# A causal attention block with a quantized linear layer on eight cores: chunk 0's O tiles get a place each, and its attention starts after half of the projections

## What is computed

```python
Q, K, V = (split_heads(x @ W.T, 16) for W in (WQ, WK, WV))       # 16 heads of 64
scores = einsum('bhqd,bhkd->bhqk', Q, K) / 8;  causal mask;  attn = softmax(scores)
x1 = layernorm(x + einsum('bhqk,bhkd->bhqd', attn, V) @ WO.T)
x_q = round(rms_norm(x1) * 127 / absmax) / (127 / absmax)        # per row, clipped to int8
out = layernorm(x1 + x_q @ (w_int8 * weight_scale).T + bias)
```

## Time and profile before

| | |
|---|---|
| median of 3 runs | 1007.29 us (1006.96 to 1008.47) |
| the profiled execution: its own time | 1006.75 us |
| its span (core 1, the slowest; others 999.1 to 1003.6) | 1004.6 us |
| PE busy | 901.4 us, 90% of the span |
| ACT busy | 677.8 us, 67% |
| DVE busy | 524.4 us, 52% |
| POOL busy | 226.8 us, 23% |
| mean DMA rate | 71 GB/s |

### The profile page before, as it was taken

One profiled execution on the slowest core, in us unless ns is written; L12 is line 12 of the kernel. 1 busy time (PEld: TensorE's weight loads), 2 busy tenths in 40 slices (PEclk: granted clock), 3 DMA queues, 4 the chain that ended last, 5 costly groups with the idle time before them and its releaser, 6 DMA issues.

```text
span 1004.6 us, 22672 instructions; the slowest of 8 cores (999.1 to 1004.6 us)
## 1 busy us (share of the span) xinstructions
PE 901.4 (90%) x8416; PEld 416.6 (41%) x8416; DVE 524.4 (52%) x1269; ACT 677.8 (67%) x707; POOL 226.8 (23%) x289
## 2 busy tenths in 40 slices
PE   3895999999999999899999999999899998888863
PEld 1342444444444444444444444444344444444431
DVE  0110147834875337752148727862577523676665
ACT  0133756777787788888834666777677778989931
POOL 5022422322222111211122322232122111121201
PEclk9997999999999999999999999999999999999987
DMA  9999141530132122241071331141313210123222
GB/s 125 149 177 205 32 54 33 106 106 12 34 85 80 49 33 48 59 106 48 7 96 38 95 117 23 47 133 54 49 33 106 80 33 9 31 65 100 59 58 63
DMA packets 99289, 71.18 MB, mean 71 GB/s; under 512 B 70384, under 2 KB 88816, under 8 KB 99184
## 3 DMA queue, kind: packets, MB, share of 16 engines
q1 hardware_dynamic: 78368, 50.87, 19.7%
q0 software_dynamic: 20816, 18.88, 14.2%
HBM read 55.05 MB, written 16.78 MB: 71 GB/s over the span
## 4 chain that ended last, share of the span: by engine, by line
PE 68%; DMA 9%; ACT 7%; DVE 6%; issue 6%; DVEq 2%; POOL 1%; POOLq 0%; ACTq 0%; SPq 0%
PE ps L322 43%; PE ps L628 13%; PE ps L529 13%; ACT PT L557 6%; DMA WV<-wvt 4%; DMA QO<-OS 3%; DVE OS L664 2%; DMA XT<-xt 1%; ACT Q L826 1%; DVE SM L760 1%; DVE Z L890 1%; DMA QT<-QB 1%; DVEq L663 1%; DVE SM L757 1%; DVE SM L763 1%
## 5 line engine op out<-in xcount | busy, mean ns | idle before, releaser
L557 ACT ACTIVATE PT<-ps,SM 128x1024 bf16<-128x1024 f32 (+2 forms) x576 | 580.6, 1066 | 179.2 <-PE ps L529 176.2
L572 POOL TENSOR_TENSOR PT<-PT,MASK 128x256 bf16<-128x256 bf16 (+1 forms) x184 | 158.2, 867 | 540.0 <-ACT PT L557 539.9
L628 PEld LDWEIGHTS ps<-VX,PT 128*128 128x128 bf16 x4352 | 186.9, 98 | 185.0 <-issue 125.0
L628 PE MATMUL ps<-VX,PT 128*128 128x65 bf16 x4352 | 231.5, 194 | 29.2 <-DVE OS L664 28.5
L529 PE MATMUL ps<-QO,KT 64*128 64x512 bf16 (+1 forms) x1504 | 186.1, 324 | 23.7 <-ACT PT L557 20.6
L322 PE MATMUL ps<-XT,WK 128*128 128x512 bf16 x512 | 131.6, 383 | 19.2 <-DMA XT<-xt 18.9
L322 PE MATMUL ps<-W,QT 128*128 128x512 bf16 x512 | 135.2, 382 | 14.8 <-DMA QT<-QB 14.5
L322 PE MATMUL ps<-WO,QO 128*128 128x512 bf16 x512 | 134.8, 378 | 3.7 <-issue 2.2
L322 PE MATMUL ps<-WV,XT 128*128 128x512 bf16 x512 | 129.6, 385 | 3.9 <-DMA WV<-wvt 3.3
L322 PE MATMUL ps<-XT,WQ 128*128 128x512 bf16 x512 | 131.5, 378 | 0.6 <-DMA WQ<-wqt 0.6
L529 PEld LDWEIGHTS ps<-QO,KT 64*128 64x128 bf16 x1504 | 53.9, 94 | 174.2 <-issue 167.9
(11 more groups left out here) (50 smaller groups left out, 549.1 us busy)
## 6 DMA issues: line engine op xcount, KB each, us to landing
Z<-x SPq DMA_DIRECT2D x32, 512.0 KB, 4.1
y<-Z SPq DMA_DIRECT2D x32, 512.0 KB, 3.1
XT<-xt POOLq DMA_DIRECT2D x7, 1024.0 KB, 11.9
WK<-wkt POOLq DMA_DIRECT2D x4, 512.0 KB, 20.4
WQ<-wqt POOLq DMA_DIRECT2D x4, 512.0 KB, 23.3
WV<-wvt POOLq DMA_DIRECT2D x2, 1024.0 KB, 41.2
WO<-wot POOLq DMA_DIRECT2D x1, 2048.0 KB, 68.2
W<-w8t POOLq DMA_DIRECT2D x1, 2048.0 KB, 83.3
```

Source lines behind the costliest of these rows:

```text
L557: emit("s", lambda eng: eng.activation(dst, src, AF.Exp, bias=EB, scale=0.125).then_inc(sem["s"], 1))
L572: emit("g", lambda eng: eng.tensor_tensor(blk, blk, msk, ALU.mult).then_inc(sem["m"], 1))
L628: last = eng.matmul(ps[:, 2048 + s_ * 512 + q * 65: 2048 + s_ * 512 + q * 65 + 65], PT[:, pt0 + s_ * 512 + c0: pt0 + s_ * 512 + c0 + 128], ...
```

## The change

It has four parts.

1. **Order of the loads.** WK and WQ come in slices of 128, 256, 256 and 384 columns (head pair 0; 1 and 2; 3 and 4; 5 to 7) in place of four of 256. V's first half is loaded after the second slices, V's second half after the fourth ones, still ahead of XT1, WO and W8. Only WK's first slice lies between the two halves of x^T.
2. **Fewer fills ahead of attention.** Ahead of the first unit come K and Q of head pairs 0 to 2 and V's first half, 10 fills. The other 14 go first in the list that is spread over chunk 0's gaps: K and Q of pair 3, V's second half (4 fills), then K and Q of pairs 4 to 7.
3. **A place for each O.** Chunk 0's head pairs 0 and 1 use OS, 2 and 3 use O6 (the place of Q16/QB), 4 to 7 use QT8; both are idle in chunk 0. The wait for the transpose of pair i-2 is gone in chunk 0.
4. **Later first rows.** The loads of x and the bias are issued ahead of unit pair 8 of 12 of chunk 0. In chunk 1 four K fills are listed ahead of the first two row blocks' WO fills.

```diff
@@ -88,6 +88,7 @@
 
         Q16 = at("Q16", [128, 1024], F16, "q16")
         QB = at("QB", [128, 1024], BF16, "q16")
+        O6 = at("O6", [128, 1024], BF16, "q16")
         QT8 = at("QT8", [128, 2048], BF16, "qt8")
         BIAS = at("BIAS", [128, 1024], F32, "bias")
         MASK = at("MASK", [128, 128], BF16, "mask")
@@ -163,19 +164,20 @@
 
         tok_xt = {}
         tok_w = {}
+
+
         x0a = xt_load(XT0, 0, 0, 4, "x0a")
-        tok_w["k", 0] = wslice(wk_h, WK, 0, 256, "wk0")
-        x0b = xt_load(XT0, 0, 4, 8, "x0b")
-        tok_w["q", 0] = wslice(wq_h, WQ, 0, 256, "wq0")
+        for j, (i0, i1) in enumerate(((0, 1), (1, 3), (3, 5), (5, 8))):
+            for w, w_h, W in (("k", wk_h, WK), ("q", wq_h, WQ)):
+                tok = wslice(w_h, W, 128 * i0, 128 * i1, "w%s%d" % (w, j))
+                for i in range(i0, i1):
+                    tok_w[w, i] = tok
+                if (w, j) == ("k", 0):
+                    x0b = xt_load(XT0, 0, 4, 8, "x0b")
+            if j == 1:
+                tok_w["v", 0] = wslice(wv_h, WV, 0, 512, "wv0")
+        tok_w["v", 1] = wslice(wv_h, WV, 512, 1024, "wv1")
         tok_xt[0] = (x0a, x0b)
-        for j in range(1, 4):
-            tok_w["k", j] = wslice(wk_h, WK, 256 * j, 256 * j + 256,
-                                   "wk%d" % j)
-            tok_w["q", j] = wslice(wq_h, WQ, 256 * j, 256 * j + 256,
-                                   "wq%d" % j)
-        for j in range(2):
-            tok_w["v", j] = wslice(wv_h, WV, 512 * j, 512 * j + 512,
-                                   "wv%d" % j)
         tok_xt[1] = (xt_load(XT1, 1, 0, 8, "xt"),)
         tok_w["o"] = wslice(wo_h, WO, 0, 1024, "wo")
         tok_w["8"] = wslice(w8_h, W8, 0, 1024, "w8")
@@ -377,7 +379,7 @@
                     lambda kk: W[:, kk * 1024 + i * 128:
                                  kk * 1024 + i * 128 + 128],
                     lambda kk: X[:, kk * 512:kk * 512 + 512],
-                    lambda: (tok_w[which, i // 2],) + tok_xt[g])
+                    lambda: (tok_w[which, i],) + tok_xt[g])
 
             def done(n):
                 en = evac_engine(state["g"])
@@ -651,9 +653,14 @@
                 pv_end = t_tok()
                 later(2000.0, lambda: xt5_load(pv_end))
             wait("v", t_tok())
-            if i >= 2:
+            if su:
                 wait("v", tok_ot[(i - 2) // 8, (i - 2) % 8])
-            o0 = (i % 2) * 512
+            out, o_row, o0 = OS, 1024, (i % 2) * 512
+            if su == 0 and i >= 2:
+
+
+                out, o_row, o0 = ((O6, 1024, (i - 2) * 512) if i < 4 else
+                                  (QT8, 2048, (i - 4) * 512))
             r0 = 168 + (i % 2) * 8
 
             def f(eng):
@@ -662,7 +669,7 @@
                                   (65, nq)))
                 eng.drain()
                 eng.tensor_tensor(
-                    ap(OS, o0, (1024, 128), (64, 2), (128, nq), (1, 64)),
+                    ap(out, o0, (o_row, 128), (64, 2), (128, nq), (1, 64)),
                     ap(ps, 2048, (4096, 128), (512, 2), (65, nq), (1, 64)),
                     ap(SM, r0, (256, 128), (4, 2), (1, nq), (0, 64)),
                     ALU.mult).then_inc(sem["v"], 1)
@@ -675,7 +682,7 @@
             key = "ot%d" % (i % 2)
             emit("y", lambda eng: eng.dma_start_transpose(
                 ap(QO, c0, (8192, 128), (128, nq), (1, 128)),
-                OS[:, o0:o0 + nq * 128]).then_inc(sem[key], 16))
+                out[:, o0:o0 + nq * 128]).then_inc(sem[key], 16))
             tok_ot[su, hp] = bump(key, 16)
             if hp == 7:
                 later(5500.0, lambda: state["ot_all"].add(su))
@@ -837,7 +844,7 @@
             later(2200.0, lambda: bg.insert(0, (400.0, integers)))
 
             def resid(j):
-                wait("v", tok_q16[n], tok_bias)
+                wait("v", tok_q16[n], tok_bias[0])
                 z = zt(n, j * 512, j * 512 + 512)
                 emit("v", lambda eng: eng.scalar_tensor_tensor(
                     z, z, sm(n, 6, 7), BIAS[:, j * 512:j * 512 + 512],
@@ -965,29 +972,30 @@
         state["ot_all"] = set()
 
         tok_consts2 = [None]
+        tok_bias = [None]
 
 
         ops["v"] = vhead
         emit("v", consts_fn)
         tok_consts2[0] = bump("v")
 
-        for i in range(8):
+        for i in range(3):
             main.append(proj_filler("k", 0, i))
             main.append(proj_filler("q", 0, i))
-        for dc in range(2):
-            for r in range(4):
-                main.append(v_filler(0, r, dc))
+        for r in range(4):
+            main.append(v_filler(0, r, 0))
         while main or st["open"]:
             step()
 
-
-        wait("y", t_tok())
-        for n in range(NZ):
-            x_load(n)
-        emit("y", lambda eng: eng.dma_start(
-            BIAS[:, :], ap(bias_h, 0, (0, 128), (1, 1024))
-        ).then_inc(sem["bi"], 16))
-        tok_bias = bump("bi", 16)
+        def first_rows(t):
+
+            wait("y", t)
+            for n in range(NZ):
+                x_load(n)
+            emit("y", lambda eng: eng.dma_start(
+                BIAS[:, :], ap(bias_h, 0, (0, 128), (1, 1024))
+            ).then_inc(sem["bi"], 16))
+            return bump("bi", 16)
 
         def chunk_list(g):
 
@@ -1016,6 +1024,8 @@
                          v[0], ff[2], v[1], v[2], v[3], ff[3],
                          v[4], v[5], v[6], v[7], q[0], q[1], q[2], q[3]]
                 late = [q[4], q[5], q[6], q[7]]
+                if g == 1:
+                    order = order[2:6] + order[:2] + order[6:]
             return sum(order, []), sum(late, [])
 
         def behind(tiles):
@@ -1024,7 +1034,12 @@
             fl += [ffn_filler(n, dc) for n in tiles for dc in range(2)]
             return fl
 
+
         carry = []
+        for i in range(3, 8):
+            carry += [proj_filler("k", 0, i), proj_filler("q", 0, i)]
+            if i == 3:
+                carry += [v_filler(0, r, 1) for r in range(4)]
         pairs = {}
         for p in range(len(units) // 2):
             pairs.setdefault(subs[units[2 * p][0]][0], []).append(p)
@@ -1072,6 +1087,8 @@
                 fill(left() / max(1, gaps[0]))
                 gaps[0] -= 1
             for p in pairs[g]:
+                if p == pairs[0][8]:
+                    tok_bias[0] = first_rows(t_tok())
                 emit_s(2 * p)
                 emit_s(2 * p + 1)
                 pv_pair(p - 1, gap)
```

## The result

The changed kernel takes 1019.35 us in the median (1018.77 to 1019.62 in the three executions that are compared); its ratio to the kernel before is **1.0111, 95% interval 1.0093 to 1.0129**: slower by some 11 us. The forecast was 1008.1, its range 1005.2 to 1011.0.

A forecast was written before the change was run, and what follows sets the result against it. PE, busy 90% of the span, was taken to bound the kernel, with the DMA engines full for the first 100 us. 1006.75 - 0.2 + 0.6 + 0.4 = 1007.55, plus 0.54 for the median, gave 1008.1 us, range 1005.2 to 1011.0.

The forecast's parts named there:

- T - S + 20.2 - W: Time change past chunk 0's waits: S is the first score matmuls, W chunk 0's old wait; -0.2 us on core 1.
- The new wait: In chunk 0, PE stands from 41.2 to 54.7 us for V's second half, about 13.5 us.
- The wait of chunk 0: PE's wait in chunk 0 for a multiply of O, itself held by a transpose, goes: -10.3 us.
- Slices of 128 columns: Loads of WK and WQ: smaller packets make V's second half land +0.6 us later, between 0 and +2.7.
- rival A: 256-byte packets cost as much as 512-byte ones or more, so V's second half lands later: 1010.2 us, chance 0.20.
- Evacuations: In chunk 0, ACT evacuates 34 fills, not 20, between the same exps: +0.4 us, bounds 0 and 4.4.
- rival B: In chunk 0, fills are evacuated on ACT behind two exps: 1012.1 us at the upper bound, chance 0.13.
- Row loads later, and chunk 1's K fills first: 0: Later loads of x and bias in chunk 0, and K fills ahead of WO fills in chunk 1, cost 0.
- One of my own signs: In the changed kernel's profile, the first WO fill at about 134 us as before; wrong if over 3 us off.
- The cores: Core 1 -0.2 us, core 5 +0.4, core 2 +2.7; the longest span stays core 1's or core 5's.
- So the end costs what it did: At the kernel's end, the last 140 pieces of PE's order are the same, so its cost is unchanged.
- Rivals C and D: C: no slow restart behind PE's wait, 1005.6 us, chance 0.09. D: V's second half lands before PE asks, 993.6, 0.04.

The follow-up runs named there:

- e4: The kernel before with only the separate places for chunk 0's O; 994.21 us, ratio 0.9879 to the kernel before.
- e3: The changed kernel with V's second-half fills listed behind K and Q of head pairs 3 to 7; 1002.86 us, ratio 0.9978.
- e1: The changed kernel with chunk 1's list as it was, WO fills of the first two row blocks ahead of K fills; 1010.41 us, ratio 1.0049.
- e2: The changed kernel with four slices of 256 columns of WK and WQ; ratio 1.0327 with cores at lower clock, so only landing times and four cores' spans count.
- e9: e4 with WK and WQ in slices of 128, 256, 256 and 384 columns, otherwise in its order of loads; 998.71 us, ratio 0.9919.
- e8: e4 with the loads of x and the bias issued ahead of pair 8 of chunk 0; 994.75 us, ratio 0.9872.
- e7: e4 with chunk 1's four K fills listed first; 1000.85 us, ratio 0.9937.
- e5: The changed kernel with V's second-half fills behind K and Q of pairs 3 to 7 and chunk 1's list as it was; 998.59 us, ratio 0.9913.

## Why the prediction was wrong

*What bounds it, and the method*: right. The difference was T - S + 20.2 - W, T being when V's second half lands. With T as measured on core 1 (11.1 + 46.6 = 57.7) it gives +2.8 us at the end of chunk 0, and the multiplies show +3.2; on core 0 +4.0, and they show +3.1; on all eight +4.5 in the mean, and they show +4.1. (The prediction counts 14 transfers up to V's second half; there are 12, and nothing hangs on it.)

*The new wait*: right in place, cause and size, 13.5 forecast, 13.7 measured, the restart included. The wait of chunk 0 gone: right; e4 shows it to be worth 12 us by itself, and e3 that the new one is worth 13.

*Slices of 128 columns*: the first step that failed, mis-sized. I took +0.6 between 0 and +2.7, from a line through packets of 512 and 1010 bytes. V's second half came 2.0 us later by them (e1 and e3 against e2, e9 against e4), up to 3.4 in the changed kernel's profiled execution, rival A's size, and the rule of the Trainium skill (DMA: Bandwidth & Descriptors, Specifications), which I had set aside for want of a row, held. The line gave 44 ns for a packet of 256 bytes, and 47 to 56 were measured; it took the share of the engines as 123%, and on core 5 it was 114%. In the kernel's time the slices cost 4.0 us (e9), since the step did not have at all that a fill waits for the whole of its slice.

*Evacuations*: +0.4 forecast, no wait of PE for ACT up to 140 us on any core; rival B did not occur.

*"Row loads later, and chunk 1's K fills first: 0"*: this is the larger step that failed. The row loads are free (e8). The K fills first cost 5.8 us (e7) to 6.5 us (e3 against e5). I asked only who waits for the loads of x, looked at the last 140 pieces of PE's order, which were the same, and not at ACT's order in chunk 1, where normalizations stand in a queue ahead of exps. One of my own signs points there: the first WO fill was to start at 134 us, on core 1 it started at 146.6, and at 133.2 in e1, which has the old order.

*The cores*: I worked the sum out for cores 1, 5 and 2 and took that of the slowest, core 1, with -0.2; over all eight cores the same sum gives +1.2 in the mean with the landings of before. Core 1, the slowest before, lost least of all (7.8 us of span), and core 0, which became the slowest, 17.5. But the kernel's time went up by about what the cores lost in the mean, 11.2 us by the ratio against 11.9 of span. So the slowest core of one execution was a poor one to carry a sum on, and no extra loss has to be put down to it. "So the end costs what it did" failed by 1.2 us in the mean.

*The whole.* The runs go from the kernel before to the changed one in steps, in us of ratio: the places -12.2 (e4); the slices +4.0 (e9); the early attention with V's second half last, V's first half loaded earlier and the later row loads -0.6 (e5), within the noise; chunk 1's K fills first +6.5 (e3); V's second half ahead of the K and Q fills of pairs 4 to 7 +13.4 (the changed kernel). Against the forecast: the two waits trade at +0.6, where I had -0.2 and 0.4 for evacuations; the slices are 3.4 above, the K fills 6.5. The steps add up to the measured 11 by how they are formed; that they are sizes of their own is shown only for the K fills, which cost 5.8, 6.2 and 6.5 us in three different surroundings.

*Rivals C and D*: matmuls behind the new wait were slow, and V landed in the order of issue: neither occurred. None of the rivals had chunk 1 in it, and rival A alone, at 1010.2, would still have been inside the range.

## What to carry to other kernels

When fills are moved among loads that come in one queue, list them in the order in which their weights land: the same 14 fills cost 13 us more in another order (e3). A long wait is removed where it arises, here by a few unused buffers (e4: 12 us), before the schedule around it is redone; each part of a change wants its own run, since all but one here were free, useless or harmful. When an order of fills changes, read the order of every in-order engine behind it: a result that is late there delays whatever stands behind it, here exps behind a normalization.

## What the runs showed of the hardware that was not expected

Packets of 256 bytes took 47 to 56 ns against 64 to 74 for 512 bytes, and the queue moved 93 to 128 in place of 140 to 166 GB/s. A wait of PE of 1.55 us left the matmuls behind it at full rate (16 in 3.61 us); one of 2.55 us left the first two so (0.59) and had four in 1.90 us behind them; one of 2.63 us had 16 in 5.30 us behind it, and one of 2.97 us 2 in 1.01. So a microsecond more of waiting can cost nearly three. But the length of the wait does not decide it alone: at the end of the changed kernel, on core 0, one of 2.89 us cost nothing beyond itself.

```profile
1004.71 3.61 PE L324 MATMUL ps<-W,QT 128*128 128x512 bf16 x16 [2.89 <-DMA QT<-QB]
```

The granted clock of the stretch that holds the end of the 13.96 us wait, on core 0, was 0.50, the lower of its two levels (1.2 of 2.4 GHz); PE was busy for 1.78 us of these 10:

```profile
50.00:60.00 10.00, 1.78 (x5) 0.70 (x6) 0.00 (x0) 0.00 (x0) 0.00 (x0) 0.50 1.15 164
```
